# Gate/up matmuls as 64x32 tiles over two steps, with the spill of token features in two halves

## The chip, the cores and the metric

The kernel runs on one core of a Trainium2 chip. The metric is the device time of one execution in microseconds (us). The kernel before takes 817.82 us (median of 3 runs, 815.83 to 820.35).

The engines: PE (TensorE) does matmuls, DVE (VectorE), ACT (ScalarE) and POOL (GpSimd) do elementwise work, SP (SyncE) issues all the DMAs that this text speaks of, on one queue.

## The reference, cut to what matters

```python
x = x + layernorm(attention(layernorm(x), Wq, Wk, Wv, Wo))     # x: 4 x 1024 x 512, float32
# second half, the FFN: hidden 512, inter 2048
gate_w, up_w, down_w = [spline_reconstruct(cp, ...) for cp in (gate_cp, up_cp, down_cp)]
h = layernorm(x)
inter = silu(h @ gate_w.T) * (h @ up_w.T)
x = x + layernorm(inter @ down_w.T)
```

The three FFN matrices are Catmull-Rom splines of few control points. The kernel uses this: `h @ gate_w.T` is done in two stages. First h is multiplied by fixed polynomial features, 16 for each of the 4 blocks of 128 hidden columns and each of 16 tiles (the "token features", z). Then a small matrix of 64 rows (4 x 16) turns a tile's z into gate and up values.

## The kernel before, in words

The attention stage ends near 402 us of the span; the change hardly touches it. The FFN stage works on 8 groups of 512 tokens. A group is 16 steps, one for each 128 of the 2048 inner units, and four steps are a quarter (`quad`, j = 0 to 3). Each engine has its own program, written by hand as `quad`, and `schedule` runs it for every group: groups 0, 1, 6 and 7 are written out, groups 2 to 5 are a loop (`Fori`) of two rounds. Engines meet by semaphores only, and each works in its program's order.

What PE does in a quarter of group g:

- `gate_up`, four times: for step n + 2, 8 matmuls into `gbank` and 8 into `ubank`. Each is 128 rows by 32 columns of the array with 512 moving columns, so four of them fill the array (a pass). The 128 rows hold z in two parts, high and low (float16 each), 64 rows each; the weights are `s_twice` (the high part of the spline weights, twice) and `s_low` (their low part).
- `moment_pair`, twice: two passes of 128x32 tiles into `mbank`.
- `part`, four times: the down projection of group g - 1, 12 matmuls of 160 columns into `ybank`, with three matmuls of 512 columns (`moment_rows`) before the first part of a quarter and three behind the last. Four parts make the output of 128 tokens. `ybank` is two banks in turn.
- `turn` and `products`: for 128 tokens of a later group (m = 4g + j + 6) the transpose of h, 8 matmuls, and 24 matmuls with the features into two banks, `zbank` and `turned`. ACT (`z_high`) and DVE (`z_low`) then write them as float16 to `z_hi` and `z_lo`.

ACT does silu from `gbank` (`silu_at`), DVE multiplies by `ubank` (`product`, four buffers `inter`), ACT rounds (`high`) and POOL takes the difference (`low`) for the down projection. `y_out`, `o_stats`, `o_scale`, `o_norm`, `o_finish` are the output's layernorm and the residual.

z has to be laid out anew, from tokens by tile to feature rows by tile, and that goes through DRAM. SP issues in a group: loads of h tiles (`x_ln`), the output stores (`finish`), the loads of the residual (`reload`, which waits until the store has left the buffer), and at j = 2 `regroup` for the next group: 8 DMAs `token_features<-z_hi/z_lo` of the first half of the tiles (`spill`), a wait until they are in memory, the load of that half of z, then the same for the second half. The features of the next group are complete with tile m = 4g + 7, that is with the second quarter (j = 1) of group g. PE's first step of group g + 1 is issued in the last quarter, at i = 14, and waits for the first half of z; there are two z buffers.

Of the kernel before, what the change touches and what calls it, by code (L numbers as in the profile page):

```python
# [881 lines left out]
class TokenFeatures:  # L882
# [4 lines left out]
    def __init__(self, ctx, nc, K, tiles, spilled):  # L887
# [40 lines left out]
        self.z_ready = sem("z_ready")  # L928
        self.z_spilled = [sem(f"z_spilled{h}") for h in range(2)]
# [6 lines left out]
    def spill(self, sp, first, last, g, buf=0):  # L936

        if first == 0:
            sp.wait_ge(self.z_ready, (g + 1) * self.Q)
        for n in range(first, last):  # L940
            half, k, part = n // (2 * self.K), n // 2 % self.K, n % 2
            sp.dma_start(self.spilled[half, part, k].rearrange("f t n -> t f n"),
                         self.z_parts[buf][part][:, half * self.K + k, :]).then_inc(self.z_spilled[half], 16)
# [20 lines left out]
    def z_high(self, act, m, q, groups_before, banks, buf=0):  # L964

        K = self.K
        if q == 0 and not (isinstance(groups_before, int) and groups_before == 0):
# [31 lines left out]
    def z_low(self, dve, m, q, banks, buf=0):  # L999
        K = self.K  # L1000
        high, low_t = self.z_parts[buf]
        for half in range(2):
# [6 lines left out]
        low.then_inc(self.z_ready, 1)  # L1009
# [12 lines left out]
    def products(self, pe, m, banks):  # L1022

        feat, hT = self.feat, self.hT
        pe.wait_ge(self.hT_copied, m + 1)
        for half in range(2):
# [9 lines left out]
class FfnInputs:  # L1036
# [41 lines left out]
    def load_z(self, sp, feats, g, par, half):  # L1078
# [3 lines left out]
        sp.dma_start(z[:, half * self.half:(half + 1) * self.half, :],  # L1082
                     feats.spilled[half].rearrange("a k f t n -> (a k f) t n")).then_inc(self.z_loaded[par][half], 16)


def ffn_block(nc, x1, feats, ffn_in, d_dram, moments, c_gate, c_up, c_out, out, id16):
# [26 lines left out]
    with ExitStack() as ctx:  # L1113
# [29 lines left out]
        gbank, ubank, tbank, zbank = [psum(n, [P, BANK], F32) for n in ("gbank", "ubank", "turned", "zbank")]  # L1143
        ybank = [psum(f"ybank{q}", [P, BANK], F32) for q in range(2)]
        mbank = [psum(f"mbank{q}", [P, BANK], F32) for q in range(2)]
        z_banks = [zbank[:], tbank[:]]
# [3 lines left out]
        gate_done = sem("gate_done")  # L1150
        up_done = sem("up_done")
# [21 lines left out]
        def schedule(engine, quad):  # L1173


            def group(g, par, count, made, begun, more):
                for j in range(Q):
                    quad(g, par, count, j, j < made, j < begun, more)

            group(0, 0, 1, Q, Q, True)  # L1180
            group(1, 1, 1, Q, Q, True)
            with engine.Fori(0, GROUPS // 2 - 2) as pair:
                for par in range(2):
                    group(2 * pair + (2 + par), par, pair + 2, Q, Q, True)
            group(GROUPS - 2, 0, GROUPS // 2, 2, 1, False)
            group(GROUPS - 1, 1, GROUPS // 2, 0, 0, False)
# [11 lines left out]
        def _(sp):  # L1198
# [15 lines left out]
            def regroup(g, par, loads_before):  # L1214


                for half in range(2):
# [4 lines left out]
            def quad(g, par, count, j, made, begun, more):  # L1222
# [4 lines left out]
                if j == 2 and not (isinstance(g, int) and g == GROUPS - 1):  # L1227
                    regroup(g + 1, 1 - par, count)
# [27 lines left out]
        def _(pool):  # L1256
# [16 lines left out]
            def quad(g, par, count, j, made, begun, more):  # L1273
                for s in range(4):
                    i = 4 * j + s
                    n = g * I + i
                    if not (isinstance(n, int) and n == STEPS - 1):
                        low(n + 1, (i + 1) % I, par if i + 1 < I else 1 - par)
# [583 lines left out]
```

## Time and profile before

| what | value |
|---|---|
| median of the runs | 817.82 us |
| profiled execution, its own time | 813.27 us |
| its span | 811.4 us |
| FFN stage | from about 408 to 811 us |
| PE busy | 740.7 us (91%) |
| DVE busy | 529.2 us (65%) |
| ACT busy | 373.7 us (46%) |
| POOL busy | 440.0 us (54%) |
| granted clock of PE, mean | 0.972 |

Busy times are of the whole span. The end of a matmul is modelled, so the distance from start to start tells what PE takes, not the duration beside it. A row of a timeline has the start, the duration, the engine, the line of the kernel, the operation, what it writes and reads, and how many such instructions were merged (x4). In brackets stands how long the engine was idle before it, and who released it.

### The profile page before, as it was taken

How to read it: one execution, taken by the hardware profiler on the slowest of the kernel's cores; microseconds unless marked ns; L12 is line 12 of the kernel's file. 1: busy time of each engine (PE TensorE's matmuls, PEld its weight loads, DVE VectorE, ACT ScalarE, POOL GpSimd, SP SyncE). 2: the span in 40 equal slices, each digit the busy share in tenths (PEclk: the TensorE clock that was granted, in tenths of full speed). 3: DMA queues.
4: the chain of work that ended last, by engine and by line, in shares of the span. 5: the costliest groups of instructions: out<-in, count | busy, mean ns of one | idle time of the engine just before them, and what ended most of it. 6: DMA issues, size and time to landing. Idle time of an engine off the chain costs nothing. (4 is left out here: it accounts for less than half of the span.)

```text
span 811.4 us, 19045 instructions
## 1 busy us (share of the span) xinstructions
PE 740.7 (91%) x7152; PEld 507.3 (63%) x7152; DVE 529.2 (65%) x1025; ACT 373.7 (46%) x635; POOL 440.0 (54%) x615
## 2 busy tenths in 40 slices
PE   6987999999999999799767899999989999999996
PEld 3665767787787768587533366565656556565565
DVE  7674763686458744565656668778767787865453
ACT  3531332343233333132446666666656666666541
POOL 5289749185854669311335446555545455455542
PEclk9897899999999999899989999999999999999999
DMA  6725447144732456502871515455353544536313
GB/s 239 267 81 174 155 165 239 55 149 133 231 126 77 142 194 235 111 2 88 271 249 57 192 59 169 140 163 178 124 178 93 180 160 131 171 105 192 109 53 105
DMA packets 64314, 120.55 MB, mean 149 GB/s; under 512 B 12144, under 2 KB 28656, under 8 KB 62192
## 3 DMA queue, kind: packets, MB, share of 16 engines
q1 hardware_dynamic: 64240, 119.53, 45.2%
q8 instruction: 51, 0.84, 0.4%
q14 instruction: 23, 0.19, 0.1%
HBM read 82.94 MB, written 36.57 MB: 147 GB/s over the span
## 5 line engine op out<-in xcount | busy, mean ns | idle before, releaser
L1260 POOL TENSOR_TENSOR act<-inter,act 128x512 f16<-128x512 f32 x128 | 158.5, 1249 | 127.2 <-ACT act L1301 127.2
L1374 DVE SCALAR_TENSOR_TENSOR inter<-ubank,c_up,gated 128x512 f32<-128x512 f32 x128 | 95.9, 749 | 74.9 <-ACT gated L1305 74.2
L1514 PE MATMUL ybank<-down,act 128*128 128x160 f16 x512 | 110.4, 235 | 0.0
L1515 PE MATMUL ybank<-down,act 128*128 128x160 f16 x512 | 109.5, 233 | 0.0
L1516 PE MATMUL ybank<-down,act 128*128 128x160 f16 x512 | 109.5, 233 | 0.0
L1305 ACT ACTIVATE gated<-gbank,c_gate 128x512 f32<-128x512 f32 x128 | 87.8, 686 | 45.3 <-PE gbank L1473 45.3
L1301 ACT CAST act<-inter 128x512 f16<-128x512 f32 x128 | 78.9, 617 | 48.8 <-DVE inter L1374 48.8
L1514 PEld LDWEIGHTS ybank<-down,act 128*128 128x128 f16 x512 | 50.1, 98 | 39.2 <-issue 35.5
L1473 PE MATMUL gbank<-z,s_twice 128*32 128x512 f16 x512 | 51.8, 395 | 9.5 <-PEq L84 4.3
L748 PE MATMUL ybank<-ga_hi,xT_hi 128*128 128x512 f32 x128 | 51.8, 404 | 6.1 <-ACT shared L539 4.4
L539 ACT ACTIVATE shared<-ybank,yr 128x512 f32<-128x512 f32 x32 | 22.0, 688 | 72.0 <-POOL yr L363 72.0
L598 DVE SCALAR_TENSOR_TENSOR tu_lo<-chain,tu_hi 128x512 fp32r<-128x512 f32 x32 | 22.1, 690 | 48.6 <-ACT tu_hi L472 48.5
L1473 PE MATMUL ubank<-z,s_twice 128*32 128x512 f16 x512 | 50.3, 383 | 3.3 <-DVE inter L1374 3.3
L1515 PEld LDWEIGHTS ybank<-down,act 128*128 128x128 f16 x512 | 50.3, 98 | 3.9 <-issue 0.3
L361 POOL TENSOR_TENSOR yr<-ymv,eps 128x1 f32<-128x1 f32 x32 | 19.9, 623 | 59.4 <-DVE ymv L675 59.4
L1473 PE MATMUL gbank<-z,s_low 128*32 128x512 f16 x512 | 50.4, 384 | 0.0
L1516 PEld LDWEIGHTS ybank<-down,act 128*128 128x128 f16 x512 | 50.3, 98 | 0.0
L1405 DVE SCALAR_TENSOR_TENSOR x_res<-y,orr,x_res 128x512 f32<-128x512 f32 x32 | 43.7, 1364 | 10.1 <-ACT y L1323 7.7
L1473 PE MATMUL ubank<-z,s_low 128*32 128x512 f16 x512 | 50.1, 381 | 0.0
L749 PE MATMUL ybank<-ga_lo,xT_hi 128*128 128x512 f32 x128 | 50.0, 391 | 0.0
L750 PE MATMUL ybank<-ga_hi,xT_lo 128*128 128x512 f32 x128 | 49.9, 390 | 0.0
L472 ACT ACTIVATE tu_hi<-chain 128x512 fp32r<-128x512 f32 x32 | 19.1, 597 | 65.6 <-PE chain L750 65.6
(192 smaller groups left out, 2076.2 us busy)
## 6 DMA issues: line engine op xcount, KB each, us to landing
x_ln<-x SPq DMA_DIRECT2D x64, 256.0 KB, 3.5
z<-token_features SPq DMA_DIRECT2D x16, 1024.0 KB, 5.4
job<-job_in SPq DMA_DIRECT2D x24, 640.0 KB, 4.1
shared<-x SPq DMA_DIRECT2D x32, 256.0 KB, 2.8
x<-shared SPq DMA_DIRECT2D x32, 256.0 KB, 2.0
token_features<-z_hi SPq DMA_DIRECT2D x64, 128.0 KB
token_features<-z_lo SPq DMA_DIRECT2D x64, 128.0 KB
x_res<-x SPq DMA_DIRECT2D x32, 256.0 KB, 2.8
```

Of the source, the lines that this page charges most:

```text
L748: pe.matmul(out, l_hi, r_hi, start=start, stop=False)
L749: pe.matmul(out, l_hi, r_lo, start=False, stop=False)
L750: return pe.matmul(out, l_lo, r_hi, start=False, stop=stop)
L1260: pool.tensor_tensor(hidden[par][:, i, TOK:2 * TOK], inter[:, i % INTERS, :], hidden[par][:, i, 0:TOK], ALU.subtract).then_inc(inter_ready, 1)
L1301: act.copy(hidden[par][:, i, 0:TOK], inter[:, i % INTERS, :]).then_inc(inter_hi_done, 1)
L1305: act.activation(gated[:, slot % 2, :], gbank[:], ACT.Silu, scale=c_gate[:]).then_inc(silu_done, 1)
L1374: dve.scalar_tensor_tensor(out=inter[:, i % INTERS, :], in0=ubank[:], scalar=c_up[:], in1=gated[:, i % 2, :], op0=ALU.mult, op1=ALU.mult). ...
L1405: dve.scalar_tensor_tensor(out=x_res[:, q % 2, :], in0=y[:, q % 2, :], scalar=orr[:, q, 2:3], in1=x_res[:, q % 2, :], op0=ALU.subtract, op ...
L1473: mm = pe.matmul(bank[rows], part[:, side, c, w, rows], z[par][:, i // 4 * 4 + u, :], start=start, stop=not start)
L1514: pe.matmul(out, hidden[par][:, r, high], box[:, 0], start=False, stop=False)
L1515: pe.matmul(out, hidden[par][:, r, high], box[:, 1], start=False, stop=False)
L1516: mm = pe.matmul(out, hidden[par][:, r, low], box[:, 0], start=False, stop=False)
```

## The change

1. `gate_up` works for two steps at once. The contraction is cut to 64 rows: a tile is 64 rows by 32 columns, eight of them fill the array, four for each of the two steps. Three products remain of four (high z by high weights, low z by high weights, high z by low weights), so a pair of steps takes 24 matmuls for gate and 24 for up. There are two gate banks and two up banks (`gbanks`, `ubanks`).
2. To make room, one output bank (`outbank`) and one feature bank (`zbank`) remain. The halves of `products` are now issued apart: the first half in the second pair of a quarter, the second half in the next quarter's first pair, behind the wait `z_half_ready`.
3. Each engine's `quad` is written in pairs of steps; `turn` stands at the end of the first pair (in group 0 behind the second `gate_up`).
4. SP spills the first half of z in the second quarter (j = 1), ahead of that quarter's `finish` and `reload`; in the third it spills the second half, and then issues both loads of z. Each load is now two DMAs of 64 partitions.
5. PE's groups are written out, with no loop.

```diff
     def z_low(self, dve, m, q, banks, buf=0, halves=(0, 1)):
...
-        low.then_inc(self.z_ready, 1)
+            low.then_inc((self.z_half_ready, self.z_ready)[half], 1)
...
-    def products(self, pe, m, banks):
+    def products(self, pe, m, banks, halves=(0, 1)):
...
-        for half in range(2):
+        for half in halves:
+            if half == 0:
+                pe.wait_ge(self.hT_copied, m + 1)
+            elif halves == (1,):
+                pe.wait_ge(self.z_half_ready, m + 1)
...
+        pairs = self.half // 2
+        for two in range(2):
+            sp.dma_start(z[64 * two:64 * two + 64, half * self.half:(half + 1) * self.half, :],
+                         feats.spilled[half][:, :, two * pairs:(two + 1) * pairs].rearrange("k f t a n -> (k f) (t a) n")
+                         ).then_inc(self.z_loaded[par][half], 16)
...
-        z_banks = [zbank[:], tbank[:]]
+        z_banks = [zbank[:], zbank[:]]
...
-            def regroup(g, par, loads_before):
-                for half in range(2):
-                    sp.wait_ge(z_loaded[1 - par][half], loads_before * 16)
-                    feats.spill(sp, half * feats.SPILLS // 2, (half + 1) * feats.SPILLS // 2, g, 1 - par)
-                    ffn_in.load_z(sp, feats, g, par, half)
+            def spill_half(g, par, loads_before, half):
+                sp.wait_ge(z_loaded[1 - par][half], loads_before * 32)
+                feats.spill(sp, half * feats.SPILLS // 2, (half + 1) * feats.SPILLS // 2, g, 1 - par)
...
-                if j == 2 and not (isinstance(g, int) and g == GROUPS - 1):
-                    regroup(g + 1, 1 - par, count)
+                if not (isinstance(g, int) and g == GROUPS - 1):
+                    if j == 1:
+                        spill_half(g + 1, 1 - par, count, 0)
+                    elif j == 2:
+                        spill_half(g + 1, 1 - par, count, 1)
+                        ffn_in.load_z(sp, feats, g + 1, 1 - par, 0)
+                        ffn_in.load_z(sp, feats, g + 1, 1 - par, 1)
...
-                for w, bank, free, done in ((GATE, gbank, silu_done, gate_done), (UP, ubank, inter_done, up_done)):
-                    if not (isinstance(n, int) and n == 0):
+                for w, banks, free, done in ((GATE, gbanks, silu_done, gate_done), (UP, ubanks, inter_done, up_done)):
+                    if not first:
                         pe.wait_ge(free, n)
-                    for part, start in ((s_twice, True), (s_low, False)):
+                        pe.sem_inc(banks_free, 1)
+                    for part, low, start, stop in ((s_twice, 0, True, False), (s_twice, 1, False, False),
+                                                   (s_low, 0, False, True)):
                         for u in range(4):
-                            rows = slice(32 * u, 32 * u + 32)
-                            mm = pe.matmul(bank[rows], part[:, side, c, w, rows], z[par][:, i // 4 * 4 + u, :],
-                                           start=start, stop=not start)
-                    mm.then_inc(done, 1)
+                            for e in range(2):
+                                rows, at = slice(64 * (u % 2), 64 * (u % 2) + 64), 32 * (u ^ e)
+                                mm = pe.matmul(banks[e][at:at + 32],
+                                               part[rows, side, (i + e) % HALF, w, 32 * u:32 * u + 32],
+                                               z[par][rows, i // 4 * 4 + u // 2 * 2 + low, :], start=start, stop=stop)
+                    mm.then_inc(done, 2)
...
-            schedule(pe, quad)
+            schedule(pe, quad, turning=False)
```

SP's queue, kernel before, from the residual load in the second quarter of a group of the loop to the first load of z in the third (`token_features<-z_hi` is a spill, `z<-token_features` the load of z, `x_ln<-x` an h tile, `out<-x_res` the store, `x_res<-x` the residual):

```order
L1204 DMA out<-x_res 128x512
...
L1200 DMA x_res<-x 128x512
...
L934 DMA x_ln<-x 128x512
...
L942 DMA token_features<-z_hi 8x16x512 [waits z_ready]
L942 DMA token_features<-z_lo 8x16x512
...
L1082 DMA z<-token_features 128x4096 [waits z_spilled0]
L942 DMA token_features<-z_hi 8x16x512 [waits z_loaded01]
...
L1082 DMA z<-token_features 128x4096 [waits z_spilled1]
```

The same place in the changed kernel:

```order
L945 DMA token_features<-z_hi 8x16x512 [waits z_half_ready]
L945 DMA token_features<-z_lo 8x16x512
...
L1224 DMA out<-x_res 128x512
...
L1220 ISA [waits out_stored0]
L1220 DMA x_res<-x 128x512
...
L935 DMA x_ln<-x 128x512
...
L945 DMA token_features<-z_hi 8x16x512 [waits z_ready,z_loaded01]
...
L1090 DMA z<-token_features 64x4096 [waits z_spilled0]
L1090 DMA z<-token_features 64x4096
L1090 DMA z<-token_features 64x4096 [waits z_spilled1]
```

The first eight spills moved ahead of the store, and the store with its wait (`out_stored0`), the residual load, two h tiles and the second eight spills now stand between them and the first load of z.

PE, kernel before, one step and the next in the loop (L1514 opens a part, L1503 to L1505 are its moment rows):

```order
L1473 MATMUL gbank<-z,s_twice 32x512 [waits silu_done]
L1473 MATMUL gbank<-z,s_twice 32x512 x3
L1473 MATMUL gbank<-z,s_low 32x512 x4
L1473 MATMUL ubank<-z,s_twice 32x512 [waits inter_done]
L1473 MATMUL ubank<-z,s_twice 32x512 x3
L1473 MATMUL ubank<-z,s_low 32x512 x4
L1489 MATMUL mbank<-act,basis 32x512 [waits mom_ready,inter_ready]
```

The same place in the changed kernel, the first pair of a quarter:

```order
L1521 MATMUL gbank<-z,s_twice 32x512 [waits silu_done]
L1521 MATMUL gbank<-z,s_twice 32x512 x15
L1521 MATMUL gbank<-z,s_low 32x512 x8
L1521 MATMUL ubank<-z,s_twice 32x512 [waits inter_done]
L1521 MATMUL ubank<-z,s_twice 32x512 x15
L1521 MATMUL ubank<-z,s_low 32x512 x8
L1036 MATMUL zbank<-hT,feat 128x128 [waits z_half_ready]
...
L1538 MATMUL mbank<-act,basis 32x512 [waits inter_ready]
```

48 matmuls of 64x32 for two steps stand where 32 of 128x32 stood, and half of the products stands between them and the moments.

## Rows read from the trace of the kernel before

**Rows 1.** Windows, one per group: PE, PEld, DVE, ACT, POOL busy, clock, DMA, GB/s.
```profile
408.06:453.29 45.23, 32.61 (x440) 14.59 (x441) 28.28 (x53) 25.47 (x44) 20.72 (x25) 0.93 0.50 161
453.29:499.67 46.38, 44.88 (x637) 27.17 (x638) 33.48 (x61) 29.39 (x51) 24.08 (x31) 1.00 0.39 132
...
548.17:596.51 48.34, 47.15 (x667) 29.17 (x666) 38.53 (x69) 31.08 (x53) 26.56 (x36) 1.00 0.48 153
...
695.74:741.06 45.32, 44.68 (x627) 26.95 (x626) 31.33 (x55) 28.68 (x48) 25.16 (x32) 1.00 0.43 140
741.06:785.50 44.44, 43.07 (x581) 24.04 (x580) 24.03 (x42) 27.00 (x44) 25.36 (x32) 1.00 0.34 104
```

**Rows 2.** Waits in the FFN stage: total us, times, longest.
```profile
PE gbank L1473 <- issue: 2.3, 1, 2.3
...
PE gbank L1473 <- DMA z<-token_features: 0.2, 1, 0.2
```

**Rows 3.** Timeline of PE, two steps of the fourth group.
```profile
572.69 0.40 PE L1473 MATMUL gbank<-z,s_twice 128*32 128x512 f16 x4
...
573.57 0.60 PE L1489 MATMUL mbank<-act,basis 128*32 128x512 f16 x8
574.10 0.24 PE L1514 MATMUL ybank<-down,act 128*128 128x160 f16 x1
...
574.94 0.22 PE L1030 MATMUL zbank<-hT,feat 128*128 128x128 f16 x1
...
576.38 0.40 PE L1473 MATMUL gbank<-z,s_twice 128*32 128x512 f16 x4
...
577.36 0.24 PE L1514 MATMUL ybank<-down,act 128*128 128x160 f16 x1
```

**Rows 4.** Timeline of SP, groups 0, 2 and 3.
```profile
439.70 0.60 SPq L942 DMA_DIRECT2D token_features<-z_hi  x1
...
447.85 0.33 SPq L1082 DMA_DIRECT2D z<-token_features  x1
...
504.22 0.33 SPq L1082 DMA_DIRECT2D z<-token_features  x1
504.60 0.43 SPq L1204 DMA_DIRECT2D out<-x_res  x1
510.31 0.33 SPq L1200 DMA_DIRECT2D x_res<-x  x1
...
576.94 0.35 SPq L1204 DMA_DIRECT2D out<-x_res  x1
579.19 0.34 SPq L1200 DMA_DIRECT2D x_res<-x  x1
579.80 0.86 SPq L934 DMA_DIRECT2D x_ln<-x  x2
580.80 0.60 SPq L942 DMA_DIRECT2D token_features<-z_hi  x1
...
585.26 0.57 SPq L942 DMA_DIRECT2D token_features<-z_lo  x1
...
590.90 0.34 SPq L1082 DMA_DIRECT2D z<-token_features  x1
```

**Rows 5.** The 15 loads of z in the FFN stage, by their line.
```profile
DMA to landing us min/median/max: 4.8/5.4/6.6
```

**Rows 6.** Timeline of PE: first gate of the third quarter, and of the next group.
```profile
578.93 0.40 PE L1473 MATMUL gbank<-z,s_twice 128*32 128x512 f16 x4
...
596.51 0.40 PE L1473 MATMUL gbank<-z,s_twice 128*32 128x512 f16 x4
```

**Rows 7.** Window behind the loop's jump, columns as in rows 1.
```profile
606.00:609.40 3.40, 3.40 (x25) 1.74 (x18) 2.30 (x4) 1.03 (x2) 0.00 (x0) 0.50 0.37 121
```

**Rows 8.** Timeline of one step of group 0: silu, and the product behind it.
```profile
426.85 0.69 ACT L1305 ACTIVATE gated<-gbank,c_gate 128x512 f32<-128x512 f32 x1 [0.86 <-PE gbank L1473]
...
427.57 0.75 DVE L1374 SCALAR_TENSOR_TENSOR inter<-ubank,c_up,gated 128x512 f32<-128x512 f32 x1 [2.23 <-ACT gated L1305]
```

More of the change, by code:

```diff
@@ new lines, in silu_pair, with high_pair, quad @@
+            def silu_pair(g, i):
+                for e in range(2):
+                    silu_at(g * I + (i + 2 + e), i + 2 + e)
+            def high_pair(g, i, par):
+                for e in range(2):
+                    if i + 2 < I:
+                        high(g, g * I + (i + 2 + e), i + 2 + e, par)
+                    else:
+                        high(g + 1, g * I + (i + 2 + e), e, 1 - par)
+            def quad(g, par, count, j, made, begun, more, owed):
+                i, m = 4 * j, g * Q + j + AHEAD
+                for before, q in outputs(g, i, 0):
+                    if q % 2 == 0:
+                        y_out(before, q)
+                silu_pair(g, i)
+                if owed:
+                    feats.z_high(act, m - 1, (j + 1) % Q, g + 1, z_banks, 1 - par if j == 3 else par, (1,))
+                if made:
+                    feats.high(act, m)
+                high_pair(g, i, par)
+                if i == 0 and not (isinstance(g, int) and g == 0):
+                    moment_hi(g - 1, 1)
+                last = isinstance(g, int) and g == GROUPS - 1 and j == Q - 1
+                if not last:
+                    silu_pair(g, i + 2)
+                if made:
+                    feats.z_high(act, m, (j + 2) % Q, g + 1, z_banks, par if j < 2 else 1 - par, (0,))
+                for before, q in outputs(g, i + 2, 2):
+                    o_norm(before, q)
+                if not last:
+                    high_pair(g, i + 2, par)
+                if j == Q - 1:
+                    moment_hi(g, 0)
@@ new lines, in product_pair, with quad @@
+            def product_pair(g, i):
+                for e in range(2):
+                    product(g * I + (i + 2 + e), i + 2 + e)
+            def quad(g, par, count, j, made, begun, more, owed):
+                i, m = 4 * j, g * Q + j + AHEAD
+                loads = g + (1 + (j + AHEAD + 1) // RING)
+                for before, q in outputs(g, i, 0):
+                    if q % 2 == 1:
+                        y_out(before, q)
+                if made:
+                    feats.norm(dve, m, (j + AHEAD) % RING)
+                product_pair(g, i)
+                if owed:
+                    feats.z_low(dve, m - 1, (j + 1) % Q, z_banks, 1 - par if j == 3 else par, (1,))
+                if made:
+                    feats.low(dve, m)
+                if begun:
+                    feats.stats(dve, m + 1, (j + AHEAD + 1) % RING, loads)
+                for before, q in outputs(g, i, 0):
+                    o_stats(before, q)
+                if i == 0 and not (isinstance(g, int) and g == 0):
+                    moment_lo(g - 1, 1)
+                if made:
+                    feats.turn_copy(dve, m, z_banks)
+                if not (isinstance(g, int) and g == GROUPS - 1 and j == Q - 1):
+                    product_pair(g, i + 2)
+                if made:
+                    feats.z_low(dve, m, (j + 2) % Q, z_banks, par if j < 2 else 1 - par, (0,))
+                for before, q in outputs(g, i + 2, 2):
+                    o_finish(before, q)
+                if j == Q - 1:
+                    moment_lo(g, 0)
```

190 lines of the change are left out of this document (81 added, 109 removed).

## The prediction, made before the changed kernel ran

> **What bounds the kernel now.** I read first the windows by group. Between the first gate matmul of one group and of the next lie 45.3 to 51.1 us, 47.96 us in the mean of the six from 453.29 to 741.06; in the fourth group PE is busy 47.15 of 48.34 us, DVE 38.53, ACT 31.08 [rows 1]. PE is the bound, and it is really streaming, not only marked busy: four passes of gate/up take 573.57 - 572.69 = 0.88 us, 0.22 each; two moment passes and what follows them 0.53; a part 0.84; 24 products with the turn to the next gate 1.44 [rows 3]. From the gate at 576.38 to the part at 577.36 are 0.98 us, which is four passes and 0.10 to 0.11 for going over from 32-column tiles to the full array [rows 3]. PE's waits are small: 2.3 us once, at the loop's jump, and 0.2 us once for z [rows 2].
>
> The second reading is SP's timeline, since PE's first step of a group needs the first half of that group's z. In the fourth group the load of z was issued at 590.90, a load lands 5.4 us later, at 596.3, and the gate that needs it started at 596.51 [rows 4 to 6]. So the way of z through DRAM is ready just as PE comes: there is no slack on it. It has three long pieces: eight spills (580.80 to about 585.8, 0.64 apart), the wait until they are in memory (until 590.90), the load (5.4 us).
>
> **The change part by part.** I call the start of the third quarter (j = 2) T. In the fourth group T was 578.93 [rows 6].
>
> *PE's work.* A quarter before: 16 gate/up passes 3.47 us, 4 moment passes 0.87, 24 products 1.35 and 8 turns 0.45 (0.056 each), four parts 3.35, six moment rows 1.30 (512 columns, as a pass), 8 changes of tile shape 0.88. That is 11.67 us, 46.7 for a group, against 48.34 measured. After: a pair of steps takes 3 passes for gate and 3 for up, if eight tiles of 64x32 share the array as four of 128x32 do. So 12 passes 2.60 us, and 7 changes of shape 0.77 (gate, products, moments, part in the first pair; gate, moments, part in the second); the rest stays. 10.69 us, 42.8 for a group. The second bank of gate and up takes away what is left of waiting for silu. By this alone a group gains 4 us and more.
>
> *Work off PE.* DVE has 38.5 us in a group of 48.3 [rows 1]; in 42.8 it would be 90% busy. In the first quarter its order is long (`moment_lo`, `y_out`, `norm`, two products, `z_low`, `low`, and only then may PE's `turn` start): I cost that at 0.9 us a group; between 0 and 2. Everything else (ACT, POOL, the pairs) fits, and it is hidden under PE's parts or under the stall below.
>
> *The way of z.* Now the same three pieces from T, in SP's new order. The first half of the last tile's features is ready when the second quarter ends (its products are issued in that quarter's last third, and `z_high` and `z_low` follow), so at about T + 0.1.
> 1. First eight spills: issued T + 0.1 to T + 5.1. In memory 8.15 us after the first issue, where nothing was ahead on the queue (439.70 to 447.85 [rows 4]): T + 8.2.
> 2. The store `out<-x_res` is issued at T + 5.1, behind them. With a free queue SP goes on 2.25 us later (576.94 to 579.19); behind a 1 MB load it took 5.7 us (504.60 to 510.31), as long as that load itself [rows 4]. So a transfer waits for those ahead of it on the queue, and the store returns about 1 us after the spills: T + 9.2.
> 3. Residual load, two h tiles: 1.6 us (579.19 to 580.80): T + 10.8.
> 4. Second eight spills: issued to T + 15.8. Behind three 256 KB loads they are in memory 10.1 us after the first issue (580.80 to 590.90), 8.15 without: T + 19.0 to T + 20.9.
> 5. The first half of z is issued at T + 15.8, but its packets stand behind the spills. 5.4 us to landing, of which 1 us is over before the queue is free: T + 23.9.
>
> PE needs it at the last quarter's second pair: 10.7 us for the third quarter and 5.6 for the first pair of the fourth, T + 16.3; before it was T + 17.6 (596.51 - 578.93). So PE comes earlier and z later, by my reading 7.6 us too late, in each of seven groups. The wait is on the first gate matmul; behind it on PE stand the moments and parts of the quarter, and all engines run dry.
>
> Bounds for this: from below, if the store returns in its free 2.25 us and z lands in 5.4 us from its issue, T + 7.4, T + 9.0, T + 14.0, T + 19.4. From above, both spills 10.1 us, no overlap: T + 28.3. I take 23.9, near the rows that have a filled queue.
>
> *The clock.* Behind the 2.3 us stop at the loop's jump the granted clock was 0.50 (the level of 1.2 GHz) for the 3.4 us from 606.00 [rows 7], which costs up to half of them, 1.7 us. A stop of 7.6 us brings at least one such stretch: 1.5 us a group; 0 to 3.
>
> *The sum.* From the landing to the next T PE has the rest of the last quarter (10.7 - 5.6 = 5.1), two quarters (21.4), 0.9 and 1.5: 28.9. With 23.9 one group takes 52.8 us, against 47.96. Six times + 4.8 is + 29; the seventh group loads no h tiles, - 1.5. First group: a step of it costs a chain of PE, silu and product, 0.72 us from silu to product [rows 8], and pairs halve the number of these chains, so I estimate two or three us less for each of the two quarters ahead of T. But from the first spill (439.70 [rows 4]) to the next group's gate (453.29 [rows 1]) were 13.6 us, and by the new order (no store in this group) they are 5 + 1 + 5 of issues and 9 until z has landed, 20. So nothing (- 3 to + 3). Last group: 16 passes fewer, 3.5 us, and one slow stretch back, 1.5: - 2. The loop's jump (2.3 us) falls into a stall and brings nothing. Output banks at the end: no wait before, none after. Together + 25 us on the profiled execution, whose own time is 813.27 and thus 4.5 below the median: 838, and 842 for the median of runs.
>
> *A rule against the new loads.* Each half of z is now two DMAs of 64 partitions. By the Trainium skill (DMA: Bandwidth & Descriptors, Rules for kernel authors) two transfers to disjoint halves of the partitions serialize on the same engines, and one of 128 partitions is to be preferred. By that the pair lands no earlier than the single load did, and the sum would stay as it is but for SP's second issue. No row of before shows a pair of halves.
>
> **The rivals.**
>
> *A, PE remains the bound.* If z is there by T + 16.3, a group takes 42.8 + 1.5 us: 6 x 3.7 = 22, the first group 3, the last 3.6: 29 us less, 789 us. For it: SP's first spills do start earlier, by 1.8 us, and the wait for them in memory is now covered by other issues. Against it: those issues are longer than the wait was (590.90 - 585.8 = 5.1 us), and the queue is one. It decides at a landing of T + 16.3.
>
> *B, the stall is half as large.* The lower bound of the landing, T + 19.4: a group takes 5.1 + 21.4 + 0.9 + 1.5 + 19.4 = 48.3, as before. 817 us. For it speaks that a store alone returns in 2.25 us; against it the 5.7 us behind a load.
>
> *C, tiles of different rows take turns.* The trace of before has only tiles of 128 rows side by side. If those of rows 0 to 63 and of 64 to 127 do not overlap, a pair takes 12 passes, 4 more than before and 1.3 us more than above; 6.5 us more from landing to T, z still late: 59.3 us a group, about 895 us. The Trainium skill (TensorEngine Tiling (Array Packing), Gotcha 1: PSUM Pressure) says that different row tiles cannot access one PSUM bank at the same time. Here u = 0 and u = 1 write one bank, at other partitions; in the same 32 partitions the two row halves always have different banks. By that rule, taken to the letter, case C would be the result; with the bank taken by partition, it would not apply.
>
> **How the numbers follow.** Forecast (z late by 4 to 11 us) 0.67, A 0.15, B 0.13, C 0.05. The likeliest gives 842; its own range, from landings between T + 21.5 and T + 26, is 826 to 860. The range for all goes down to 796, into A, and up to 862, and leaves out most of A and C, some 0.18. What a measurement here can tell from no change is 0.5%, 4 us: faster 0.19 (A and a third of B), same 0.07, slower 0.74 (forecast, C and the rest of B).
>
> **What would show it.** Right: PE waits for the DMA `z<-token_features` at the first gate of groups 1 to 7, 4 us or more each; intervals between first gates of 50 to 55 us; a half clock behind each; on SP more than 8 us from the first spill of the second quarter to the residual load; passes of eight tiles 0.22 us apart. Wrong: no such wait, with intervals near 44 us (A); waits near 3 us (B); gate of a pair longer than 0.7 us from first matmul to up (C). If DVE is what PE's `turn` waits for in each quarter, my 0.9 us was too small.

## The result, and the profile after

The changed kernel takes 857.82 us (median of 4 runs, 856.92 to 860.91); the kernel before took 816.83 us beside it (median of 4). The ratio is 1.051, with a 95% interval of 1.047 to 1.055: 41 us slower. The forecast was 842 us, within 796 to 862.

The profiled execution took 860.91 us, 47.6 more than that of before. The first gates of the groups split it: 2.1 us fall ahead of the first gate, 48.1 into the seven intervals between the first gates of groups 0 to 7, and the end is 2.5 us shorter. The 2.1 us are no effect that can be laid on the change: e1, e3, e4 and e8 below run the same program up to the first gate, which starts at 407.4 to 408.8 us in them and at 410.2 here. The intervals are 50.6, 54.0, 56.1, 55.0, 56.6, 55.3 and 53.5 us. The waits of PE in the FFN stage, to set against [rows 2] (total us, times, longest):

```profile
PE gbank L1521 <- DMA z<-token_features: 68.9, 7, 13.0
PE zbank L1021 <- DVE h_lo L995: 10.3, 9, 1.5
PE gbank L1521 <- PEq L84: 6.2, 1, 6.2
```

Seven waits for z of 9.8 us in the mean, where there was one of 0.2. The windows show the fourth group (first gate to first gate), the work of one quarter in it without a stall (two pairs of steps), and the stretch in which the clock was low:

```profile
core 0: us, PE busy (x) PEld busy (x) DVE busy (x) ACT busy (x) POOL busy (x), PEclk, DMA share, GB/s
570.88:625.87 54.99, 44.97 (x792) 28.96 (x793) 37.02 (x68) 29.41 (x52) 27.31 (x36) 0.90 0.48 137
584.89:595.54 10.65, 10.65 (x200) 7.06 (x198) 9.77 (x20) 7.28 (x13) 6.04 (x9) 1.00 0.22 71
619.73:629.97 10.24, 4.10 (x60) 1.51 (x61) 1.20 (x2) 1.27 (x2) 0.14 (x1) 0.50 0.93 216
```

A quarter's work without a stall takes 10.65 us and PE is busy in all of it. So the tile change saves what was worked out, and the group loses more than that at its one stall (8.96 us here). PE's timeline at full clock shows the new tiles at work (start, duration, line, instruction):

```profile
589.94 0.62 PE L1521 MATMUL gbank<-z,s_twice 64*32 64x512 f16 x16
590.39 0.40 PE L1521 MATMUL gbank<-z,s_low 64*32 64x512 f16 x8
590.60 0.61 PE L1521 MATMUL ubank<-z,s_twice 64*32 64x512 f16 x16
591.03 0.40 PE L1521 MATMUL ubank<-z,s_low 64*32 64x512 f16 x8
591.36 0.23 PE L1036 MATMUL zbank<-hT,feat 128*128 128x128 f16 x1
```

24 matmuls of 64x32 take 0.66 us (589.94 to 590.60), three times 0.22: eight of them share the array, as four of 128x32 did [rows 3]. The other 24 and the change of shape take 0.76.

The same engine at the stall, in the fourth group, of which T (first gate of the third quarter) is 600.59:

```profile
616.30 0.39 PE L1021 MATMUL zbank<-ident,h_hi 128*128 128x128 f16 x4
616.52 0.39 PE L1021 MATMUL zbank<-ident,h_lo 128*128 128x128 f16 x4
625.87 1.05 PE L1521 MATMUL gbank<-z,s_twice 64*32 64x512 f16 x16 [8.96 <-DMA z<-token_features]
626.68 0.67 PE L1521 MATMUL gbank<-z,s_low 64*32 64x512 f16 x8
627.11 1.10 PE L1521 MATMUL ubank<-z,s_twice 64*32 64x512 f16 x16
```

PE is through at 616.9, T + 16.3, stands for 8.96 us, and then takes 1.24 us for what takes 0.66 at full clock. And SP, to set against [rows 4]:

```profile
600.57 0.65 SPq L945 DMA_DIRECT2D token_features<-z_hi  x1
...
604.98 0.57 SPq L945 DMA_DIRECT2D token_features<-z_lo  x1
605.66 0.43 SPq L1224 DMA_DIRECT2D out<-x_res  x1
609.77 0.35 SPq L1220 DMA_DIRECT2D x_res<-x  x1
610.39 0.86 SPq L935 DMA_DIRECT2D x_ln<-x  x2
611.35 0.61 SPq L945 DMA_DIRECT2D token_features<-z_hi  x1
...
616.31 0.64 SPq L945 DMA_DIRECT2D token_features<-z_lo  x1
617.44 4.26 SPq L1090 DMA_DIRECT2D z<-token_features  x4
621.82 0.52 SPq L1224 DMA_DIRECT2D out<-x_res  x1
```

The first half of z is written first and loaded last: between its last spill and its load stand a store, the wait for that store (4.1 us, until 609.77), two loads and eight more spills. The load then needs longer than the 5.4 us of before [rows 5]; to landing, minimum, median and maximum of the line:

```profile
DMA to landing us min/median/max: 5.9/7.6/9.7
```

### The profile page after: what moved, and what is told of

Its sections match the earlier page's. It is cut to its first block, busy times and chain, and to the rows that moved or that the text cites. A ratio compares the mean times of both kernels' runs of the same rounds, so it can differ in the third digit from the quotient of the medians.

```text
span 859.1 us, 21259 instructions
## 1 busy us (share of the span) xinstructions
PE 721.5 (84%) x8176; PEld 505.9 (59%) x8176; DVE 525.7 (61%) x1025; ACT 364.5 (42%) x635; POOL 445.2 (52%) x615
## 2 busy tenths in 40 slices
DMA packets 64577, 120.66 MB, mean 140 GB/s; under 512 B 12400, under 2 KB 28912, under 8 KB 62448
## 4 chain that ended last, share of the span: by engine, by line
issue 17%; PE 13%; POOL 10%; SPq 4%; DMA 4%; DVE 3%; ACT 1%; POOLq 0%; DVEq 0%; ACTq 0%
POOL act L1283 7%; SPq L945 3%; DMA z<-token_features 3%; PE gbank L1521 2%; PE ubank L1521 2%; PE mbank L1538 1%; PE outbank L1566 1%; PE outbank L1567 1%; PE outbank L1568 1%; POOL orr L1292 1%; POOL hr L959 1%; DMA out<-x_res 1%; DVE inter L1414 1%; DVE z_lo L1007 1%; PE zbank L1036 1%
## 5 line engine op out<-in xcount | busy, mean ns | idle before, releaser
L1283 POOL TENSOR_TENSOR act<-inter,act 128x512 f16<-128x512 f32 x128 | 163.5, 1297 | 205.5 <-ACT act L1328 205.5
L1414 DVE SCALAR_TENSOR_TENSOR inter<-ubank,c_up,gated 128x512 f32<-128x512 f32 x128 | 89.9, 743 | 91.6 <-ACT gated L1334 91.2
L1334 ACT ACTIVATE gated<-gbank,c_gate 128x512 f32<-128x512 f32 x128 | 81.1, 686 | 134.7 <-PE gbank L1521 133.9
L1521 PE MATMUL gbank<-z,s_twice 64*32 64x512 f16 x1024 | 44.3, 418 | 75.7 <-DMA z<-token_features 68.9
L1566 PE MATMUL outbank<-down,act 128*128 128x160 f16 x464 | 100.2, 236 | 0.0
L1567 PE MATMUL outbank<-down,act 128*128 128x160 f16 x464 | 100.1, 236 | 0.0
L1568 PE MATMUL outbank<-down,act 128*128 128x160 f16 x464 | 99.9, 236 | 0.0
L1521 PEld LDWEIGHTS gbank<-z,s_twice 64*32 64x32 f16 x1024 | 9.3, 90 | 93.3 <-issue 90.6
L1007 DVE SCALAR_TENSOR_TENSOR z_lo<-zbank,z_hi 128x512 f16<-128x512 f32 x54 | 37.0, 685 | 35.2 <-ACT z_hi L975 35.2
L1566 PEld LDWEIGHTS outbank<-down,act 128*128 128x128 f16 x464 | 46.0, 99 | 17.4 <-issue 14.0
L975 ACT ACTIVATE z_hi<-zbank 128x512 f16<-128x512 f32 x54 | 32.5, 601 | 55.5 <-PE zbank L1038 52.1
L1567 PEld LDWEIGHTS outbank<-down,act 128*128 128x128 f16 x464 | 46.0, 99 | 3.4
L1568 PEld LDWEIGHTS outbank<-down,act 128*128 128x128 f16 x464 | 46.1, 99 | 0.0
L748 PE MATMUL chain<-z_hi 128*128 128x512 f16 (+3 forms) x128 | 37.9, 307 | 8.0 <-DVE z_lo L583 8.0
```

Source lines behind the costliest of these rows:

```text
L748: pe.matmul(out, l_hi, r_hi, start=start, stop=False)
L1007: low = dve.scalar_tensor_tensor(out=low_t[:, half * K:(half + 1) * K, q * P:(q + 1) * P], in0=banks[half].rearrange("p (k n) -> p k n", n=P),
L1283: pool.tensor_tensor(hidden[par][:, i, TOK:2 * TOK], inter[:, i % INTERS, :], hidden[par][:, i, 0:TOK], ALU.subtract).then_inc(inter_ready, 1)
L1334: act.activation(gated[:, slot % 2, :], gbanks[slot % 2][:], ACT.Silu, scale=c_gate[:]).then_inc(silu_done, 1)
L1414: dve.scalar_tensor_tensor(out=inter[:, i % INTERS, :], in0=ubanks[i % 2][:], scalar=c_up[:], in1=gated[:, i % 2, :], op0=ALU.mult, op1=AL ...
L1521: mm = pe.matmul(banks[e][at:at + 32], part[rows, side, (i + e) % HALF, w, 32 * u:32 * u + 32], z[par][rows, i // 4 * 4 + u // 2 * 2 + low ...
```

## The experiments

The theory: the time went because z comes late, and z comes late because its first half waits in SP's program for the second. Rivals: the new tiles cost something; the two DMAs of 64 partitions cost all; the store's wait costs all. The time of a run is the median of its executions, its ratio is to the kernel before in the same session, and T is the first gate of the third quarter, as in the prediction.

**e1: new tiles, old order of SP.**

```diff
-                    if j == 1:
-                        spill_half(g + 1, 1 - par, count, 0)
-                    elif j == 2:
-                        spill_half(g + 1, 1 - par, count, 1)
-                        ffn_in.load_z(sp, feats, g + 1, 1 - par, 0)
-                        ffn_in.load_z(sp, feats, g + 1, 1 - par, 1)
+                    if j == 2:
+                        for half in range(2):
+                            spill_half(g + 1, 1 - par, count, half)
+                            ffn_in.load_z(sp, feats, g + 1, 1 - par, half)
```

> The changed kernel with the old order of SP alone: both spills in the third quarter (j = 2), each half of z loaded as soon as its spill is in memory. Theory (z's way through DRAM, in the new order of SP's queue, is what PE waits for; T is the start of the third quarter): the first spill is issued at about T + 5 (store and its wait, residual, two h tiles first), in memory at T + 14, z lands 7.6 us later at T + 22, not T + 25. PE needs it at T + 16.3, so waits near 5 to 6 us a group instead of 9.9: 6 x 3.5 to 4 us less, 830 to 838 us. Rival (one feature bank and pairs make the features themselves late, and the order on SP matters little): no change, 855 to 860 us.

830.12 us, ratio 1.015 (1.009 to 1.022), at the fast end of what was expected. The order alone is 28 of the 41 us. But z is late in the old order too, where PE comes sooner than it did and the loads are in halves. In the fourth group the first spill is issued at T + 5.8 us, before it was T + 1.9, since the store ahead of it goes out just behind T and not 2 us before it:

```profile
PE gbank L1519 <- DMA z<-token_features: 41.9, 7, 7.1
```

**e2: old tiles, new order of SP.** The kernel before with the spill of the first half at j = 1, the second spill and both loads at j = 2.

> The kernel before with the new order of SP alone: first spill in the second quarter, second spill and both loads of z in the third; tiles, banks and PE's program are those of before. Theory: z lands at about T + 23 to T + 24 (one DMA a half), PE needs it at T + 17.6: it waits about 6 us in each of seven groups and has a stretch of half clock behind each, 6 to 7 us a group more than before: 855 to 865 us, as slow as the changed kernel, though not one matmul was changed. Rival (the loss comes from tiles and banks): 817 us, no change.

871.96 us, ratio 1.066 (1.059 to 1.073), above the expected 855 to 865; waits for z of 45.2 us in seven. z comes at T + 25.1 in the fourth group, not at T + 23 to T + 24. The new order costs some 54 us with the old tiles. The rival that the tiles are what slows the kernel falls: with this order the old tiles are some 14 us slower than the new ones.

This run also prices the halves in the new order, since its loads are single ones behind the same queue:

```profile
620.54 0.59 SPq L942 DMA_DIRECT2D token_features<-z_lo  x1
621.30 4.06 SPq L1082 DMA_DIRECT2D z<-token_features  x2
...
627.59 0.62 PE L1476 MATMUL gbank<-z,s_twice 128*32 128x512 f16 x4 [7.60 <-DMA z<-token_features]
```

From the issue of the load to the gate that waited for it are 6.3 us here (6.1 to 6.8 in the last six of the seven), and 8.4 us in the changed kernel (617.44 to 625.87; 8.4 to 9.2).

**e3: the changed kernel, the first half loaded in the second quarter.**

```diff
                     elif j == 2:
                         spill_half(g + 1, 1 - par, count, 1)
-                        ffn_in.load_z(sp, feats, g + 1, 1 - par, 0)
                         ffn_in.load_z(sp, feats, g + 1, 1 - par, 1)
+                early = j == 1 and not (isinstance(g, int) and g == GROUPS - 1)
                 for i in range(4 * j, 4 * j + 4):
                     for before, q in outputs(g, i, 2):
                         finish(before, q)
+                        if early:
+                            ffn_in.load_z(sp, feats, g + 1, 1 - par, 0)
+                            early = False
                         reload(before, q)
+                if early:
+                    ffn_in.load_z(sp, feats, g + 1, 1 - par, 0)
```

> The changed kernel, with the load of z's first half moved from behind the second spills into the second quarter, between the store out<-x_res and its wait. Theory: first spills in memory at T + 8.2, the load issued then, landing 5.4 to 7.6 us later behind the store, at T + 14 to T + 17, when PE needs it at T + 16.3: waits of 0 to 1 us, 44 to 46 us a group, 790 to 802 us. Rival (features late, PE's own program longer than 48 us a group): 840 us or more.

799.34 us, ratio 0.976 (0.969 to 0.982): faster than both. Moving one load up to the quarter before brings 58 us. Of the seven waits three are left, the longest at the end of group 0:

```profile
PE gbank L1526 <- DMA z<-token_features: 11.6, 3, 8.1
```

**e4: no way of z at all.** The changed kernel without the spills of the FFN stage; the loads fetch the features that the attention stage wrote.

> The changed kernel without the spills of z in the FFN stage: SP waits for z_half_ready and z_ready as before but issues none of the 16 DMAs token_features<-z of a group, and each group's z is loaded from what the attention stage has written, so only the first group's output is computed from its own features. Theory: no wait for z is left, and PE's program sets the pace: 42.8 us for a group and 0.9 to 1.5 us of small waits, so 44.3 between first gates, 785 to 795 us in all. Rival (the new tiles, or the single banks, are what costs): 815 us or more even so.

784.49 us, ratio 0.959 (0.953 to 0.965), groups 1 to 5 of 44 to 46 us, in one of them PE busy 43.21 of 44.60. So with z out of the way nothing in tiles or banks makes the kernel slow. It is not quite the least that PE's own work allows: e12 below, with all its spills, takes 4 us less. Why e4's groups are the longer ones is open.

**e5: the kernel before, each z load as two of 64 partitions.**

```diff
-        sp.dma_start(z[:, half * self.half:(half + 1) * self.half, :],
-                     feats.spilled[half].rearrange("a k f t n -> (a k f) t n")).then_inc(self.z_loaded[par][half], 16)
+        for a in range(2):
+            sp.dma_start(z[64 * a:64 * a + 64, half * self.half:(half + 1) * self.half, :],
+                         feats.spilled[half, a].rearrange("k f t n -> (k f) t n")).then_inc(self.z_loaded[par][half], 16)
```

> The kernel before, with each load of z cut into two DMAs of 64 partitions and nothing else changed. Theory (a pair of 64-partition DMAs brings the same bytes slower than one of 128, as the landing of 7.6 us instead of 5.4 in the changed kernel may show): z's first half lands 1 to 2 us later, the kernel before had no slack, so up to 2 us a group: 822 to 832 us. Rival (the longer landing in the changed kernel is only the queue ahead of it): 817 us, no change.

830.69 us, ratio 1.018 (1.011 to 1.024). The same bytes in two halves cost 15 us here. The median landing goes from 5.4 [rows 5] to 6.6 us, the longest from 6.6 to 9.2, and since before had no slack that is seven waits (below). Together with e2, where a single load reaches the gate 2.1 us sooner than the pair, this makes the halves a second term of the loss: over seven groups 2.1 us are 15, an estimate, since the new tiles with single loads were not run in a form that tests it. Beside e1 the run says more: with the old order and loads in halves the old tiles take 830.7 us and the new ones 830.1, so while z sets the end of a group the new tiles are worth nothing.

```profile
PE gbank L1474 <- DMA z<-token_features: 11.7, 7, 2.8
```

In the trace a packet of 8 KB, of which these loads consist, takes 577 to 581 ns in the mean in e5, in the changed kernel and in e3, against 417 ns before and 371 in e2. Whether the two DMAs or their 64 partitions do it is not shown: no run has two loads of 128 partitions.

**e8: the store and its wait behind the z loads.** The changed kernel, with `rows = {1: (), 2: range(4, 12)}.get(j, range(4 * j, 4 * j + 4))` in place of the four steps of each quarter.

> The changed kernel with the first output store, its wait and the residual load moved behind both loads of z; spills and loads stand as in the changed kernel. Theory: in the changed kernel SP waits 4.1 us for that store, which stands behind the spills on the queue. Without it the second spills start at T + 6 and are issued by T + 11; but the queue is now what they wait for (two times 5.5 us of spills and 2 to 3 us of h tiles), so z lands near T + 21 to T + 22.5 instead of T + 25.3: 3 to 4 us a group less in six groups, 832 to 840 us. Rival (the queue's own work decides, SP's wait costs nothing): no more than 1 us a group, 850 us or more.

836.04 us, ratio 1.026 (1.019 to 1.032), as expected: the store, its wait and the residual load are worth 22 us at this place, e3 brings 58. In the fourth group the load of z is issued at T + 11.7 us instead of T + 16.9, but z is there at T + 21.4 instead of T + 25.3: the 5.2 us on SP give 3.9, as the load now needs 9.8 us to the gate instead of 8.4. That the rest of e3's gain is the second half's spills, which no longer stand ahead of the load, is by subtraction.

**e9 and e6: one load of 128 partitions for each half.** With the changed kernel's layout in DRAM a single DMA has the two halves as its outermost dimension.

```diff
-        pairs = self.half // 2
-        for two in range(2):
-            sp.dma_start(z[64 * two:64 * two + 64, half * self.half:(half + 1) * self.half, :],
-                         feats.spilled[half][:, :, two * pairs:(two + 1) * pairs].rearrange("k f t a n -> (k f) (t a) n")
-                         ).then_inc(self.z_loaded[par][half], 16)
+        sp.dma_start(z[:, half * self.half:(half + 1) * self.half, :],
+                     feats.spilled[half].rearrange("k f (two t) a n -> two (k f) (t a) n", two=2)
+                     ).then_inc(self.z_loaded[par][half], 16)
```

> The changed kernel with each half of z loaded by one DMA of 128 partitions instead of two of 64, nothing else. Theory: the landing of z's first half becomes 1 to 2.5 us shorter, in each of seven groups: 842 to 852 us. Rival (only the queue ahead counts): 856 to 860 us.

1022.68 us, ratio 1.251 (1.245 to 1.258); e6, the same on top of e3, 1039.76 us.

> The kernel with the early load (load of z's first half between the first store of the second quarter and its wait), and each half of z in one DMA of 128 partitions. Theory: the landing falls from 6.7 us to 5 to 5.5 us, SP has two issues fewer, the waits for z in the first and last group (11.6 us in all) become 2 to 4 us shorter, and the h tiles and residuals behind the loads come earlier: 790 to 797 us. Rival (only the queue ahead counts): 799 us as before.

Both expectations missed, and neither run tests the halves. The first gate of a group in the middle of e9, and windows of the stretch ahead of it, from the issue of its load on and where that load is alone (columns as above):

```profile
642.67 1.06 PE L1519 MATMUL gbank<-z,s_twice 64*32 64x512 f16 x16 [24.57 <-DMA z<-token_features]
```

```profile
619.22:640.00 20.78, 0.00 (x0) 0.00 (x0) 0.10 (x1) 0.00 (x0) 1.60 (x6) 0.57 0.21 79
632.00:636.00 4.00, 0.00 (x0) 0.00 (x0) 0.00 (x0) 0.00 (x0) 0.00 (x0) 0.50 0.13 53
```

The DMA share is 0.21 over the whole stretch, and 0.13 where the load is alone: two of 16 engines, and the outermost dimension of this DMA is 2. The Trainium skill (DMA: Bandwidth & Descriptors, How many engines (k)) says that the number of engines is the largest up to 16 that divides the slowest dimension of both patterns. The 2 agrees. The spills' destination has 8 outermost, and while they are alone on the queue of the changed kernel the share is 0.53:

```profile
604.00:605.50 1.50, 1.50 (x23) 1.50 (x22) 1.50 (x3) 1.03 (x3) 0.91 (x1) 1.00 0.53 183
```

That gave the next edit: features in the bank ordered feature first, so that a spill goes out as it lies, with 16 outermost ("wide spills" from here on).

```diff
-            sp.dma_start(self.spilled[half, k, :, :, part].rearrange("f t n -> t f n"),
+            sp.dma_start(self.spilled[half, k, :, :, part],
                          self.z_parts[buf][part][:, half * self.K + k, :]).then_inc(self.z_spilled[half], 16)
...
-    halves = [t.reshape(P, K, 2, T // 4, 2, FEATURES).swapaxes(3, 4) for t in (high, low)]
+    halves = [t.reshape(P, K, 2, T // 4, 2, FEATURES).transpose(0, 1, 2, 5, 4, 3) for t in (high, low)]
```

**e14: the changed kernel with these spills alone.**

> The changed kernel with one change, the same spills with outermost dimension 16. Theory: the way of z is serial in this order, so each piece of it that gets shorter shortens the group: first spills in memory about 2 us earlier, store and residual load behind them too, the load of z no longer behind eight spills on the queue; z lands at about T + 21 to T + 22.5 instead of T + 25.3, wait 5 to 6.5 us in place of 9, and 7 x 3 us = 20 less: 832 to 842. Rival (number of engines is not what limits the spills): 855 to 860.

829.54 us, ratio 1.015 (1.011 to 1.018): 28 us less than the changed kernel, a little more than the 16 to 26 expected. Two things became quicker. In a stretch of 1.5 us the spills move at 257 instead of 183 GB/s, with a DMA share of 0.80 instead of 0.53, and SP needs mostly 0.45 us instead of 0.57 to issue one:

```profile
584.00:585.50 1.50, 1.50 (x40) 0.91 (x28) 1.50 (x3) 1.33 (x4) 1.50 (x2) 1.00 0.80 257
```

```profile
PE gbank L1521 <- DMA z<-token_features: 42.5, 7, 8.6
```

In the fourth group (T = 583.15) the first eight spills still take 5.1 us to issue, as one of them took 1.83. What is shorter is the wait for the store, 2.3 us instead of 4.1, and the second eight spills, 3.8 us instead of 5.6; z is there at T + 22.3 instead of T + 25.3, with a wait of 6.0 us, both as expected.

The number of engines can also be counted. The profile has 12400 packets under 512 B in the changed kernel and 13424 in e14: 1024 more, which is 128 spills times 8. In e9 there are 11920, 480 fewer: 32 loads times 16 less 16 loads times 2. That fits one small packet for each DMA and engine, with 8 engines for the old spills, 16 for the wide ones and 2 for the loads of e9.

**e12: wide spills and early load.**

> The early load (e3) and besides spills whose outermost dimension is 16 (features stored feature-major in the bank, so that no transposition of the spill is needed). In the changed kernel and in e3 a spill's outermost dimension is 8, the spills move some 186 KB/us (0.69 us for 128 KB) and the DMA engines are about half busy; e9 showed a DMA with an outermost dimension of 2 on 2 of 16 engines. Theory (the queue, not SP's issue, carries the rest of the stall in the early version): a spill moves in 0.35 to 0.4 us, SP's issue of 0.6 us sets the pace, the queue is clear 1 to 3 us earlier in each half, group 0 waits 4 to 6 us for z in place of 8.1, the x_ln and x_res waits of DVE shrink: 789 to 797 us against 799. Rival (SP's own issue time and the number of packets already set the pace, or the writes of 1 KB cost the same on any number of engines): no change, 797 to 802.

780.36 us (6 runs), ratio 0.954 (0.952 to 0.957), better than expected and the best version: 36.6 us faster than before, 77 faster than the change as it was made. The 19 us over e3 are not z's alone: PE's waits for z fall from 11.6 us to 4.3, and DVE's waits for h tiles and residuals, which share the queue, from 26.8 us to 5.7. How much each brings was not separated. The group is PE's own time now:

```profile
536.54:580.42 43.88, 42.82 (x794) 28.23 (x792) 37.90 (x72) 29.38 (x52) 27.37 (x37) 1.00 0.62 177
```

```profile
PE gbank L1526 <- DMA z<-token_features: 4.3, 2, 4.1
```

42.82 us of PE is the 42.8 of the prediction, in 43.9 of a group. From T to the gate of the next group are 16.25 us in five of seven groups, the PE-bound value; in the changed kernel 23.6 to 27.0. SP in the fourth group (T = 564.17):

```profile
564.15 0.33 SPq L945 DMA_DIRECT2D token_features<-z_hi  x1
...
568.06 0.45 SPq L945 DMA_DIRECT2D token_features<-z_lo  x1
568.62 0.39 SPq L1224 DMA_DIRECT2D out<-x_res  x1
569.92 1.09 SPq L1090 DMA_DIRECT2D z<-token_features  x2
571.30 0.35 SPq L1220 DMA_DIRECT2D x_res<-x  x1
```

The first half's load is out 5.8 us after T, where in the changed kernel it was 16.9.

**e16 and e15: what are the new tiles worth, and had the kernel before any slack?** e16 is e12 with the old tiles, banks and single loads; e15 is the kernel before with the wide spills alone.

> The tiles, banks and single z loads of the kernel before, with the new SP order, the early load of the first half and the wide spills: e12 without the new tiles. It says what the tiles are worth once z is in time. Theory (PE is the bound in both, by 4.0 us of matmul and tile changes a group and 3.5 us in the last): groups of 47 to 48.3 us, 780 + 6 x 3.9 + 3 + 3.5 = 810, 805 to 815 us. Rival (the tiles bring little, e12's gain on before is the queue's): 780 to 795.

> The kernel before with one change, its spills with outermost dimension 16. Theory (before, PE is the bound and z comes just in time, so a quicker way of z only makes slack): z lands about 2 us earlier than PE needs it, groups stay at 47 to 48.3 us, 811 to 817 us. Rival (some of a group's 48 us is hidden lateness of the queue): groups near 46.7 us, the sum of PE's work, 805 to 810.

808.79 us for e16 (ratio 0.991, 0.989 to 0.993) and 808.84 us for e15 (0.991, 0.989 to 0.992). By its time alone e15 falls where the rival put it, 805 to 810, and not at 811 to 817; its groups decide against the rival. The order brings nothing to the old tiles once the spills are wide: groups 2, 3 and 5 (without the loop's jump) take 48.2 to 48.5 us in both, as before. The first is e15's fourth group, the second e16's:

```profile
545.34:593.51 48.17, 47.08 (x666) 29.14 (x665) 38.34 (x69) 30.91 (x53) 26.51 (x36) 1.00 0.49 155
```

```profile
545.12:593.28 48.16, 47.07 (x666) 29.13 (x664) 38.34 (x69) 30.90 (x53) 26.50 (x36) 1.00 0.47 155
```

So with z in time the new tiles, with their banks, pairs and written-out groups, are worth 28 us (808.8 to 780.4), 4.3 us a group; the tiles alone were not run. Of e15's 7.6 us under before (ratio and medians), its profile shows 3.2 ahead of the first gate and none in the seven intervals: 332.95 us against 333.00. The attention stage's spills of group 0 use the same code, but that they bring the 3.2 is not shown: e2, which is before's program up to that gate, reaches it 1.7 us earlier than before did. The profiled execution of before was one of its shortest. Its runs beside e15 and the other experiments lay between 812.8 and 824.0 us (in several sessions), those of e15 between 808.6 and 809.4: a kernel in which z comes just in time has runs in which it doesn't. That is argued and not shown, since only one trace of before was taken.

Put together (medians):

| SP's order, spills | old tiles, single loads | new tiles, loads in halves |
|---|---|---|
| old | 817 (before) | 830 (e1) |
| old, wide spills | 809 (e15) | not run |
| new | 872 (e2) | 858 (after) |
| new, wide spills | not run | 830 (e14) |
| new and early load | not run | 799 (e3) |
| new, early load, wide spills | 809 (e16) | 780 (e12) |

## Why the prediction was right, and where its sizes were off

**The mechanism** was the one forecast: z is late on SP's queue, by the new order, and the wait is on the first gate of groups 1 to 7. e3 takes just that away and the loss is gone. None of the rivals came: A (no wait) and B (waits near 3 us) fall by seven waits of 8.7 to 13.0 us, C by passes of 0.22 us. What was off are sizes: 41 us came where 25 were forecast, near the upper end of the range.

**PE's work**: 10.69 us for a quarter, 10.65 measured; 42.8 for a group, 42.82 in e12. PE was to need z at T + 16.3, and it is through at T + 16.3. The 0.9 us for DVE in the first quarter fits e12's 43.9 a group (1.1 above PE's sum).

**The way of z**, step by step in the fourth group. Steps 1 and 2 had the store back at T + 9.2, and the residual load is issued at T + 9.2 (609.77). Step 3 had T + 10.8, and the second spills start at T + 10.8 (611.35). Step 4 had T + 15.8, and the load of z is issued at T + 16.9 (617.44): some spills took 0.64 to 0.82 us to issue where I had put 0.6 for each, and the load came 0.5 us behind the last one. That is 1.1 of the 1.4 us by which the landing was missed, T + 25.3 instead of T + 23.9. Step 5 looks right, 8.4 us from the first issue to the gate against 8.1, but by luck: I took the single load's 5.4 us from [rows 5] and let the queue add 2.7. With a single load behind this queue it was 6.3 us (e2), so the queue adds some 0.9, and the halves, which I had put at nothing, 2.1. Two errors of near 2 us cancelled. In the other groups the landing was at T + 23.6 to T + 27.0.

**The rule against the new loads** was weighed in the prediction, but left the sum as it was, by "no earlier than the single load". That was wrong: the pair lands later, by 2.1 us a group beside e2, and e5 shows 15 us by itself in the kernel before. The Trainium skill's advice (DMA: Bandwidth & Descriptors, Rules for kernel authors) to prefer the transfer over all partitions agrees with it. I should have given it a price.

**The clock**: I put 1.5 us a group for one stretch like that of [rows 7], 3.4 us long. The stretches measured were 6.8 to 13.7 us, 10.24 in the window above. But 6.1 us of that one fell into the stop, and only the 4.1 behind the gate could cost, up to 2.05 us. From gate to next T e12 needs 27.6 to 28.1 us (groups 1 to 6; the clock is 1.00 in the window above), the changed kernel 29.0 to 30.5, so clock and restart together are about 2 us a group, against the 1.5 forecast.

**The sum**: groups 1 to 6 took 55.1 us in the mean (330.46 over six), not 52.8, made up of 1.4 from the landing and 0.8 between gate and T in the group shown. And the first group was put at nothing (- 3 to + 3), but took 5.4 us more. The way from its first spill, 20 us by my steps, took 22.9 (437.91 to 460.77), and the first two quarters gave back 3.9 us from first gate to first spill (27.74 against 31.64), not 4 to 6. With six groups at 7.1 us, the first at 5.4, 2.1 ahead and 2.5 less at the end, that is 47.7 on the profiles, where I had 25. The median rose by 41, since before's profiled execution was a short one and that of after a long one; that the forecast missed the median by 16 us and not by 23 is luck of these two executions.

## What to carry to other kernels

- A queue and the program that fills it are one serial resource. Starting a chain's first piece sooner gains nothing if its last piece (here the load that someone waits for) goes behind the other pieces; ask at each issue point what is ready by now and whose result is needed first. Here one line moved by a quarter was worth 58 us.
- A faster bound engine moves its deadlines forward too. New tiles were worth 28 us with z in time (e12 beside e16) and nothing in the old order with z late (e1 beside e5); where a transfer lands just in time, price every edit on it, a split in halves too.
- Look at the outermost dimension of both sides of each DMA. A share of the DMA engines that stands near 1/8 or 1/2 while one kind of transfer is alone (0.13 and 0.53 here) is a sign that it does not use all of them.

## What the runs showed of the hardware that I had not expected

- The same 1 MB with an outermost dimension of 2 let the gate start 23.4 us after its issue (619.22 to 642.67 in e9); as two DMAs of 64 partitions it was 8.4 us in the changed kernel, as one of 128 partitions with all engines 6.3 us in e2.
- SP needs mostly 0.45 us to issue a spill with 16 outermost and 0.57 with 8. Eight took 4.4 us in e12 (564.15 to 568.5) against 5.0 in the changed kernel (600.57 to 605.6), but 5.1 in e14, where one of them took 1.83.
- A packet of 1 KB, of which the spills consist, takes 51 ns in the mean in the changed kernel and 48 in e14: the wide spills have more engines at work, not quicker packets.
- Loads to 64 partitions each take longer packets, 577 to 581 ns in the mean for 8 KB, than a load to 128, 371 to 417 (e2 and before).
- With a stop of 9 us the granted clock was 0.50 (1.2 GHz) for 10.24 us, and this began within the stop (619.73, PE had been silent since 616.9); after the 2.3 us of the loop's jump it was so for 3.4 us [rows 7].
